# The mixing stage without its 76 filler products

## What is computed

```python
x = x + layernorm(attn(layernorm(x), w_qkv, b_qkv, w_out, b_out))
x = x + layernorm(ffn(layernorm(x), W1, W2, W3))

# attn: q, k, v = split(x @ w_qkv.T + b_qkv); rope on q and k; causal softmax(q k / 4) v; @ w_out.T + b_out
# ffn:  hidden = silu(x W1') * (x W3'); hidden = fwht(hidden); out = hidden W2'
```

## Time and profile before

| what | value |
|---|---|
| median of 3 runs | 474.33 us (473.59 to 474.59) |
| the profiled execution: its time | 476.22 us |
| its span | 474.3 us |
| PE (TensorE matmul) busy | 413.7 us, 87% |
| PEld (weight loads, beside PE) | 342.5 us, 72% |
| DVE / ACT / POOL busy | 61% / 47% / 40% |
| mean granted TensorE clock | 0.948 |

### The profile page before, as it was taken

The page is one execution under the profiler, slowest core; times in us unless marked ns, Lnnn a source line. Parts: engine busy times, 40 slices in busy tenths (PEclk is TensorE's granted clock), DMA queues, the critical chain, the costliest instruction groups (busy, mean ns, idle before and its releaser), DMA issues.

```text
span 474.3 us, 8011 instructions
## 1 busy us (share of the span) xinstructions
PE 413.7 (87%) x2910; PEld 342.5 (72%) x2910; DVE 288.1 (61%) x927; ACT 223.1 (47%) x341; POOL 187.5 (40%) x313
## 2 busy tenths in 40 slices
PE   5675896899899998999999989998899989758992
PEld 4464865458699985577899965587899865537991
DVE  7547987458747678358478676487476771451114
ACT  5425458763433248834342368634232478232321
POOL 7627712743513226617122256335122265032232
PEclk9886777999999999999999999999999999979996
DMA  8647000100687000202873002004960002000001
GB/s 233 232 152 160 0 1 2 45 1 1 175 227 176 1 1 19 72 1 84 213 204 78 2 0 90 1 1 150 253 133 2 1 1 90 2 0 0 1 1 44
DMA packets 32264, 33.81 MB, mean 71 GB/s; under 512 B 1889, under 2 KB 31329, under 8 KB 32225
## 3 DMA queue, kind: packets, MB, share of 16 engines
q1 hardware_dynamic: 32224, 33.30, 25.5%
HBM read 20.19 MB, written 13.11 MB: 70 GB/s over the span
## 4 chain that ended last, share of the span: by engine, by line
PE 64%; DVE 9%; POOL 8%; DMA 7%; ACT 6%; issue 3%; SPq 1%; POOLq 0%; DVEq 0%; ACTq 0%
PE ps L310 33%; PE ps L507 9%; PE ps L495 7%; PE ps L523 7%; DMA q_t<-qk_scratch 6%; DMA qk_scratch<-qk_s 2%; POOL hid_s L945 2%; ACT probs L771 2%; POOL rstd_z L918 1%; PE ps L597 1%; PE ps L557 1%; SPq L337 1%; PE ps L460 1%; DVE masked_scores L1104 1%; PE ps L566 1%
## 5 line engine op out<-in xcount | busy, mean ns | idle before, releaser
L1104 DVE CUSTOM_DVE_ANT_0 masked_scores<-ps,mask_row 128x128 bf16<-128x128 f32 (+3 forms) x256 | 115.5, 488 | 36.9 <-PE ps L495 36.1
L310 PE MATMUL ps<-xt,w_s 128*128 128x256 f32 x768 | 109.6, 287 | 1.0 <-DVE xt L1065 0.9
L310 PEld LDWEIGHTS ps<-xt,w_s 128*128 128x128 f32 x768 | 102.0, 193 | 3.6 <-DVE xt L1065 3.0
L945 POOL TENSOR_TENSOR hid_s<-gate,hid_s 128x512 fp32r<-128x512 f32 x32 | 41.1, 1284 | 132.8 <-ACT hid_s L783 132.8
L495 PE MATMUL ps<-k_t,q_t 96*128 96x128 f32 (+3 forms) x256 | 73.3, 361 | 9.3 <-DMA q_t<-qk_scratch 5.1
L771 ACT ACTIVATE probs<-ps 128x1280 f32<-128x1280 f32 x64 | 76.1, 1238 | 10.3 <-PE ps L507 9.7
L507 PEld LDWEIGHTS ps<-q_t,k_t 128*128 128x128 f32 x256 | 44.2, 195 | 30.8 <-ACT probs L771 14.8
L310 PE MATMUL ps<-w_s,hid_s 128*128 128x256 f32 x384 | 55.0, 289 | 4.1 <-POOL hid_s L945 3.7
L507 PE MATMUL ps<-q_t,k_t 128*128 128x512 f32 (+3 forms) x256 | 54.4, 338 | 4.0 <-ACT probs L771 2.2
L495 PEld LDWEIGHTS ps<-k_t,q_t 96*128 96x128 f32 x256 | 45.6, 210 | 16.8 <-DVE maxima L1104 7.0
L310 PEld LDWEIGHTS ps<-w_s,hid_s 128*128 128x128 f32 x384 | 50.5, 192 | 6.5 <-POOL hid_s L945 6.2
(11 more groups left out here) (122 smaller groups left out, 567.6 us busy)
## 6 DMA issues: line engine op xcount, KB each, us to landing
qk_scratch<-qk_s SPq DMA_DIRECT2D x28, 256.0 KB, 4.0
k_t<-qk_scratch SPq DMA_DIRECT2D x14, 384.0 KB, 5.2
q_t<-qk_scratch SPq DMA_DIRECT2D x7, 768.0 KB, 8.7
qk_scratch<-qk_s SPq DMA_DIRECT2D x7, 512.0 KB, 3.0
xa<-in_x SPq DMA_DIRECT2D x4, 512.0 KB, 9.8
xy<-in_x SPq DMA_DIRECT2D x4, 512.0 KB, 3.4
out<-xy SPq DMA_DIRECT2D x8, 256.0 KB, 2.3
o_t<-in_w SPq DMA_DIRECT2D x1, 1024.0 KB, 9.9
```

The lines of the kernel that those rows point to most:

```text
L310: ins = eng.matmul(o, lhs(i), rhs(j), start=first and n == 0, stop=last and n == 2, skip_group_check=skip)
L945: pool.tensor_tensor(hid_s[:, a % 2, 1, :], gate[:, a % 2, :], hid_s[:, a % 2, 0, :].bitcast(F32), ALU.subtract).then_inc(S["hid_l"], 1)
L1104: ins = dve.tensor_tensor_reduce(masked_scores[:, SCORE_NO[n] % 2, i * keys:(i + 1) * keys], ps[:, banks[n], i * keys:(i + 1) * keys], mas ...
```

## The change

Every token `i0` leaves TensorE's two lists: twelve in `MIX`, in four groups of three, and two single ones in `MIX_LAST`. With two products to a token that is 24 products in each of three batches and 4 in the last, 76 in all, with the wait for `normed` ahead of each token. Nothing else moves; the lists of ACT, DVE, POOL and SP are as they were.

```diff
 MIX = {
-    "PE": """q0 o0 o1 n0 o2 o3 n1 y0 b0 n2 y1 n3 y2 q1 b1 r0 q2 y3 b2 r1 q3 r2 i0 i0 i0 b3 i0 i0 i0 H0
-        r3 H1 i0 i0 i0 u0 H2 u1 i0 i0 i0 H3 u4 u5 u2 u3""".split(),
+    "PE": """q0 o0 o1 n0 o2 o3 n1 y0 b0 n2 y1 n3 y2 q1 b1 r0 q2 y3 b2 r1 q3 r2 b3 H0
+        r3 H1 u0 H2 u1 H3 u4 u5 u2 u3""".split(),
...
 MIX_LAST = {
-    "PE": """o0 o1 n0 n1 o2 y0 n2 o3 y1 n3 y2 i0 y3 H0 H1 i0 u0 H2 u1 u4 H3 u2 u3 u5""".split(),
+    "PE": """o0 o1 n0 n1 o2 y0 n2 o3 y1 n3 y2 y3 H0 H1 u0 H2 u1 u4 H3 u2 u3 u5""".split(),
```

## The result

The changed kernel is slower. Over ten runs of each its median is 477.62 us against 475.03 us for the kernel before; the ratio is 1.0056, with a 95% interval of 1.0033 to 1.0079, that is 2.65 us (1.6 to 3.8). The forecast was 1.9 us slower, with 474.0 to 479.3 us as its range. A ratio leaves out runs more than 1.5% above the fastest of their kernel, here 479.3 and 480.9 us of the kernel without group four.

The account below looks back on a forecast made before the run. TensorE, with 64% of the chain that ended last, was taken to bound the kernel. Batch terms 0.6 + 0.6 + 0.1 + 0.4 = +1.7, plus 0.2 for longer low clock, gave +1.9 on 474.33: 476.2 us, range 474.0 to 479.3.

Parts of the forecast that it names:

- All 72 fillers are worth 0.73 us at full clock: First three batches: with the clock held, removal saves down(0)'s waits of 0.16 and 0.57 us in the first two, nothing else.
- The covers: First mixing stage: DVE's list sets when r3 and u0 start, so removing fillers ahead of them gains nothing.
- The clock falls in each of the three stages: First three mixing stages: eight transposes in 5.8 us are too little work; 1.2 GHz by u0's start or soon after.
- 4.8 us of steady work at the low level, 1.9 us lost: After the clock falls: full speed returns after 3.2 to 6.8 us, 4.8 taken; 0.39 of it lost, 1.9 us (1.25 to 2.65).
- Slow transposes, 0.1 us: Each of the first three mixing stages: transposes in r3 and H1 at the low clock may add 0.1 us.
- +0.6 for the end of u3, and for each of the first two batches: u3 ends 0.6 us later per batch (0 to +1.4); down(0) waits for that chain in batches one and two.
- the covered rival: Mixing stages: clock falls but returns after 3.2 us, u3 ends as before; 474.3 to 475.2 us, chance 0.17.
- +0.1 for the third, since it has 0.8 us to spare: Third batch: TensorE's 1.40 us wait at unit 0 leaves 0.8 us spare, so delay is nothing or up to +0.6.
- +0.4 for the last batch: Fourth batch: without its four fillers steady products begin later, so the clock returns later; 0.4 us lost, 0 to 1.3.
- Sum: Whole kernel: the batch delays and 0.2 us for longer low clock make +1.9 us, giving 476.2 us.

Follow-up runs that it names:

- last batch filled: The kernel before with nine more filler tokens in the last batch, seven ahead of H0 and two ahead of H1; ratio 0.9981 (0.9958 to 1.0004).

## Why the prediction was right, point by point

*All 72 fillers are worth 0.73 us at full clock.* The covers held. r3 did not move (4.96 us after r2 with and without), u0 did not move in a stage whose clock fell only behind r3 and H1 (7.12), and H3 came 0.98 us earlier with group four gone. Where the clock was held with group four out of the way, down(0) came 0.6 us earlier in the sum of three. But 0.73 us is no ceiling. With groups four, or one and four, gone it came 0.3 to 0.8 us earlier in each of four stages with a full clock, two of them in one execution each time. It starts 2.82 us behind unit 0 there, so the gain follows the fetch of q_t, and the third batch has its share like the others.

*The clock falls in each of the three stages.* Held, in both profiles of the changed kernel, from 128.0, 227.0 and 325.9 in the first. The pauses between the transposes were at most 2.10 us long. The rule of the Trainium skill (TensorE: Matmul & The Clock Gate, closing table), which speaks of idle stretches between bursts, would have let these pass. Read as the only way to lose the clock, it does not agree with these traces, where the clock fell in six stages of six.

*4.8 us of steady work at the low level, 1.9 us lost.* From u0 to the return of the clock it was 3.0, 4.3 and 5.0 us in the first profile and 3.9, 5.1 and 5.8 in the second, 4.5 in the mean. The forecast's 3.2 to 6.8 us covers these but for the shortest. Its share lost, 0.39, was a little low: the 15 matmuls behind it have two short transposes among them. u0's six took 1.45 us up to the next row at the low level and 0.82 at the full one, a share of 0.43. The two errors nearly cancel: 4.5 x 0.43 = 1.9.

*Slow transposes, 0.1 us.* Too small where the clock falls ahead of r3. Then u0 comes 7.47 us after r2 in place of 7.12: 0.35 us, in three stages of six.

*+0.6 for the end of u3, and for each of the first two batches.* u3's last matmul came 0.04 us earlier and then 0.9 and 1.2 us later in the first profile, and 0.7, 0.9 and 1.2 later in the second, 0.8 in the mean. Down(0) moved with it: the first batch had -0.04 and +0.7, the second +0.9 and +0.9. In the first profile's first batch the covered rival came true: full speed was back at 131.4, unit 0 still waited 0.59 us for q_t, and down(0) came as before.

*+0.1 for the third, since it has 0.8 us to spare.* This is the step that failed most. It had +1.2 in both profiles against 16.93 (+0.4 against the 17.76 that the forecast started from). The 0.8 us were read off one execution in which q_t came late; in the second profile of the kernel before, unit 0 of that batch starts 13.37 us after r2 and not 14.93. The spare time was an accident of that fetch and not a property of the batch. In four profiles of kernels with all 72 fillers in place (the kernel before twice, "last batch filled", and "only the last batch's fillers gone") the fetch was late in the third batch twice.

*+0.4 for the last batch.* Failed, the other way: 57.60 and 57.82 us after, 57.45 and 57.97 before, and no change with those four products alone taken out. The pause ahead of H0 stands behind the first two of them, and the clock falls in it with and without them.

*Sum.* +1.9 forecast, +2.65 measured (1.6 to 3.8). With the third batch at +0.6 like its neighbours and the last at 0, the same working gives 0.6 x 3 + 0.2 = +2.0; the slow transposes at 0.35 in half of the stages, not 0.1 in each, add 0.2. The two profiles have +2.0 and +2.9 over three batches against 50.8. That the sum came near is in part luck: the third batch was 1.1 us short and the last 0.4 us too much. And 0.7 us of the 1.4 between 476.2 and the measured 477.62 lie in the base, a median of three runs at 474.33 where ten gave 475.03.

## What to carry to other kernels

Before a filler is taken out, ask two things: what its own engine would do in that time, and what else hangs on the engine being busy. Here its busy time was free at full clock in three places of four, and its worth was that the products behind it ran at 2.4 GHz. Fillers belong where the engine waits for something anyway, with full-width products, and early enough to run at the high clock: behind the fall a group of six took 2.7 us in place of 1.56. And spare time that is read off a DMA wait in one trace should be looked at in a second one before a sum leans on it.

## What the runs showed of the hardware that was not expected

- At the low clock, fillers come to stand in the way: six products of 512 columns ran for 2.7 us, where at the full clock they took 1.56, and u0 came 1.3 to 1.7 us late behind them.
- Instructions alone do not hold the clock: 72 products of 64 columns in the place of 72 of 512 let it fall to 0.50 in each of three stages.
- A wait of 1.49 or 1.70 us for a DMA, behind 3 us of dense products, was followed by 3.4 us at 0.50; a wait of 1.40 us in another execution was not.
- The fetch of q_t lets unit 0 start 13.3 to 15.2 us after r2 in kernels and batches where nothing ahead of it differs, and the start-up of one and the same kernel reaches r2 of the first mixing stage at 120.94 or 122.81 us.
